# Picked columns of a graph network: who takes them out of PSUM, and how many there are

## The chip, the cores and the metric

The kernel runs on one core of a Trainium2 chip. The time is the device time of one execution in microseconds (us). Five engines work side by side, each through its own list of instructions in order: TensorE (PE) multiplies matrices into PSUM, VectorE (DVE) and ScalarE (ACT) work on PSUM and SBUF, GpSimd (POOL) issues here nothing but indirect DMAs, and SyncE (SP) issues the plain DMAs. They wait for each other by semaphores.

## The reference

Four graph networks run one after the other over one graph with 12,500 nodes and 412,500 edges, and after each comes a residual sum and a layer norm:

```
x = LN(x + L0(x))   # sum of x[src] * edge_weight * weight over the edges of each dst
x = LN(x + L1(x))   # twice: message = (MLP(edge_attr) as a 16x16 matrix) @ h[src], mean over dst, GRU cell
x = LN(x + L2(x))   # two attention layers (3 heads, 1 head): softmax over the edges of each dst
x = LN(x + L3(x))   # two relational layers, 8 edge types, mean per type
```

The edges are sorted by dst. Every layer therefore needs the rows of a node table at the edges' sources (`table[src]`), multiplies them by something of the edge, and sums them over runs of equal dst.

## The kernel before

The edges lie as 128 partitions x 3,224 columns. They are passed over seven times (`k` = 0 to 6: L0; L1 twice; L2 twice; L3 twice), each time in 62 chunks (`c`) of `TC` = 52 columns. In each pass the rows of the node table at the sources of a chunk come into `gb` in two ways:

- Most columns, `TC - OFF[k]` of them, are **gathered**: POOL issues one indirect DMA a column (`gathers`, L532), which fetches one table row for each partition.
- The last `OFF[k]` columns are **picked**. The node table lies packed in SBUF: a 32-bit word of a node's value and a word of extra bits, as bf16 halves (`pack`). For one column PE multiplies a one-hot matrix (which of 128 node groups the source lies in) with the packed table, 7 matmuls for each part of the table, into a buffer of PSUM (`pick_words`, L768). The result holds the words of 14 neighbouring nodes. DVE multiplies it by a mask that is 1 at the node wanted (`keep_words`, L1160 for tables in two parts and L1164 for one) and writes bf16 halves to `xT48` / `xT16` / `xT32`; a sum over the 14 finishes the pair of columns (`place_words` L1170, `node_words` L1194), and `decode` restores the values. The masks are made once a chunk (`word_masks`, L1144).

Columns are picked in pairs `n` of two columns `u`. In pass 0 the one-hot matrices are computed, 4 of 7 groups by DVE (`code`, L1131) and 3 by ACT (`code_far`, L639 and L642), and most are stored in DRAM (`oh_d`); passes 1 to 6 load them from there, one DMA of 448 KB a pair (`load_onehots`, L375). `KEPT` is how many pairs of a chunk are stored.

DVE then does the sums of the chunk, one scan for each value (`sums`, L1284), and between the scans it does the picks of the *next* chunk. How many picks stand before which scan is set by shares: `until(c, f)` is the number of pick steps that are due when the fraction `f` of chunk `c` is done. PE's loop in the message network (`message_net`) and SP's loads use the same shares. PE fills up to three buffers of PSUM ahead (two halves of one buffer in passes 1 and 2) and waits on `d_keep`, which DVE raises with each column kept. POOL waits on `d_gbfree` for a free half of `gb`, and every fifth gather on `d_keep`, so that it is never more than about two columns ahead of DVE's share of the chunk (`LEAD` = 2).

In the typed passes 5 and 6 each pair goes on: DVE writes its node rows (`d_row`), PE transposes them (`turn_pair`, L808 and L809), ACT copies them out (`row_copy`, L657), PE multiplies by the matrices of the eight types (`typed_product`, L799), and in pass 5 ACT copies the result (`typed_out`, L664). In passes 3 and 4 ACT has one exponential a chunk (`exp_edges`, L650); in passes 1 and 2 it makes the hidden units of the edge network (`hidden_units`, L627). In pass 0 POOL also issues 4 x 49 look-ups of another search (`find`, L519).

## Time and profile before

| | |
|---|---|
| median of the timed runs | 22,273.71 us (22,271.88 to 22,275.55, three runs) |
| span of the profiled execution | 30,666.4 us |
| PE busy | 19,689.1 us (64%), 89,726 matmuls |
| DVE busy | 18,344.5 us (60%) |
| ACT busy | 2,899.0 us (9%) |
| POOL busy | 16,237.0 us (53%) |

The profiled execution is the only one whose instructions are known; the result lists no time for it beside its span. It is 8,393 us longer than the median of the runs that were timed without a profile. Durations of single instructions and their order are read from it; how much each engine idles in it is not the same as in a timed run. In the rows, a name like `xT<-psB,sub` says what an instruction writes and reads, "idle before" is the time that the engine stood still in front of it, and what follows the arrow is what ended that.

### The profile page before, as it was taken

Reading aid. Unit: us, or ns where it says so; the run is one execution under the profiler, and the core shown is the slowest. Engines: PE = TensorE matmul, PEld = TensorE weight load, DVE = VectorE, ACT = ScalarE, POOL = GpSimd, SP = SyncE. Lnnn points to the kernel's source line nnn. Section 1 sums busy time; section 2 is a strip of 40 time slices with the busy share of each in tenths; the row PEclk is TensorE's granted clock in tenths of the full one; section 3 lists DMA queues with packets and bytes.
Section 4 is the critical chain, followed back from the end, with each engine's and each line's share of the span. In section 5 each row is a group of like instructions: output and inputs, shape, how many; then the busy total and the mean of one; then the engine's idle time right before and its main releaser. Section 6 shows DMA issues by size and latency. Waiting matters only on the chain.

```text
span 30666.4 us, 276253 instructions
## 1 busy us (share of the span) xinstructions
PE 19689.1 (64%) x89726; PEld 9475.3 (31%) x89726; DVE 18344.5 (60%) x38447; ACT 2899.0 (9%) x6609; POOL 16237.0 (53%) x16846
## 2 busy tenths in 40 slices
PE   4466657767567776455555477777566665777775
PEld 1122223333223333233333233333333333333332
DVE  6566657777567777456666465555455554555554
ACT  3344400000000000100000000000000000000000
POOL 5555555555455555445555555555355554454555
PEclk8788878888778888677777688888688886888887
DMA  3333322222122222133333122222233332222221
GB/s 122 83 103 104 101 52 66 68 66 66 45 62 68 66 68 67 32 85 88 85 86 91 45 77 76 76 76 76 62 93 93 93 91 66 55 55 55 56 56 44
DMA packets 1271680, 2237.21 MB, mean 73 GB/s; under 512 B 386665, under 2 KB 737274, under 8 KB 1261818
## 3 DMA queue, kind: packets, MB, share of 16 engines
q1 hardware_dynamic: 729380, 2025.85, 19.9%
q0 software_dynamic: 538944, 192.26, 6.7%
q8 instruction: 744, 12.19, 0.2%
q14 instruction: 670, 5.49, 0.1%
q10 hardware_dynamic: 1942, 1.43, 0.0%
HBM read 1597.46 MB, written 620.66 MB: 72 GB/s over the span
## 4 chain that ended last, share of the span: by engine, by line
DVE 36%; another core or an unknown queue 27%; PE 22%; DVEq 7%; issue 7%; POOL 1%; DMA 0%; ACT 0%; ACTq 0%; SPq 0%; POOLq 0%
PE psB L768 17%; DVE Sb L1284 6%; DVE xT L1164 5%; DVE prod L1325 5%; DVE xT L1160 4%; DVE sub L1170 4%; DVEq L1169 3%; PE psB L839 2%; DVE prod L1328 1%; DVEq L1193 1%; DVE arena L1131 1%; DVEq L1324 1%; PE psB L905 1%; PE psA L799 1%
## 5 line engine op out<-in xcount | busy, mean ns | idle before, releaser
L768 PE MATMUL psB<-xp,arena 128*128 128x476 bf16 x26040 | 6949.8, 421 | 3618.6 <-DVE xT L1164 2521.8
L768 PEld LDWEIGHTS psB<-xp,arena 128*128 128x128 bf16 x26040 | 2630.0, 108 | 7599.1 <-issue 5550.5
L768 PE MATMUL psB<-ext,arena 128*128 128x308 bf16 (+1 forms) x17388 | 3670.7, 366 | 1826.4 <-issue 1114.7
L1160 DVE TENSOR_TENSOR xT<-psB,XT 128x616 bf16<-128x616 f32 (+1 forms) x1860 | 1803.2, 977 | 3128.9 <-remote 2508.0
L532 POOL DMA_INDIRECT gb<-tab3b,typi x2356 | 2269.1, 963 | 2348.7 <-DVE xT L1160 1489.5
L532 POOL DMA_INDIRECT gb<-tab1b,srci x2356 | 2293.3, 973 | 1929.0 <-issue 645.4
L532 POOL DMA_INDIRECT gb<-tab1a,srci x2356 | 2297.1, 975 | 1905.3 <-issue 651.3
L532 POOL DMA_INDIRECT gb<-tab2a,srci x2232 | 2111.8, 946 | 2047.6 <-DVE xT L1160 1350.0
L532 POOL DMA_INDIRECT gb<-tab2b,srci x2356 | 2229.3, 946 | 1789.9 <-DVE xT L1160 1043.6
L1164 DVE TENSOR_TENSOR xT<-psB,sub 128x476 bf16<-128x476 f32 x2976 | 1920.1, 646 | 2039.8 <-remote 1670.1
L532 POOL DMA_INDIRECT gb<-tab3a,typi x2108 | 2093.8, 993 | 1897.2 <-DVE xT L1164 1015.9
L768 PEld LDWEIGHTS psB<-ext,arena 128*128 128x128 bf16 x17388 | 1791.3, 105 | 3674.4 <-issue 2432.4
L1325 DVE TENSOR_TENSOR prod<-psB,gb 128x1024 f32<-128x1024 f32 x1612 | 1974.6, 1225 | 1512.9 <-remote 1245.8
L839 PE MATMUL psB<-w2as,hid 64*128 64x256 f32 x12896 | 2119.9, 451 | 1132.1 <-DVE prod L1325 603.1
L532 POOL DMA_INDIRECT gb<-in_x,srci x1984 | 1891.0, 953 | 1655.5 <-DVE xT L1164 1011.3
L768 PE MATMUL psB<-ext,hid 128*128 128x308 bf16 (+1 forms) x8652 | 1842.0, 365 | 959.4 <-issue 575.5
L768 PE MATMUL psB<-arena,ext 128*128 128x476 bf16 x8120 | 1887.5, 389 | 798.5 <-DVE xT L1160 681.4
L1170 DVE TENSOR_REDUCE sub<-xT 128x34 f32<-128x476 f32 (+2 forms) x2418 | 1882.3, 778 | 227.0 <-issue 8.4
L839 PEld LDWEIGHTS psB<-w2as,hid 64*128 64x128 f32 x12896 | 1325.2, 214 | 2131.6 <-issue 1539.8
L1328 DVE TENSOR_REDUCE prod<-prod 128x64 f32<-128x1024 f32 x1488 | 1798.9, 1209 | 0.0
L1284 DVE TENSOR_TENSOR_SCAN Sb<-psA,Sb,prod 128x52 f32<-128x52 f32 x6588 | 1675.0, 313 | 17.2 <-issue 0.4
L1164 DVE TENSOR_TENSOR xT<-psB,arena 128x476 bf16<-128x476 f32 x1116 | 678.1, 642 | 1371.6 <-remote 1128.7
(337 smaller groups left out, 19385.5 us busy)
## 6 DMA issues: line engine op xcount, KB each, us to landing
arena<-oh_d SPq DMA_DIRECT2D x1861, 448.0 KB
hid<-oh_d SPq DMA_DIRECT2D x639, 448.0 KB
oh_d<-arena SPq DMA_DIRECT2D x558, 448.0 KB
ext<-oh_d SPq DMA_DIRECT2D x290, 448.0 KB
S2a<-Sb SPq DMA_DIRECT2D x62, 1404.0 KB
S2b<-Sb SPq DMA_DIRECT2D x62, 884.0 KB
ext<-in_attrT SPq DMA_DIRECT2D x404, 128.0 KB
S3a<-Sb SPq DMA_DIRECT2D x62, 832.0 KB
```

The costliest lines, as they stand in the source:

```text
L532: pool.indirect_dma_start(gb[:, o:o + width], None, table, at(idx[:, t:t + 1])).then_inc(l_gat[k][c % 2], 16)
L768: m = pe.matmul(psB[b][:, o:o + W], pk.onehot(n)[:, g, u * P:(u + 1) * P], pk.part(g, q).bitcast(BF16), start=g == 0, stop=g == NB - 1)
L799: t = pe.matmul(outs[u], pk.xT[0:K, o + u * P:o + (u + 1) * P], pk.mats, start=True, stop=True)
L839: m = pe.matmul(psB[g % 2][:, to:to + 256], hid[64 * u:64 * u + 64, o:o + P], w2as[64 * u:64 * u + 64, 256 * u:256 * u + 256], start=True, ...
L905: m = pe.matmul(psB[made % 3][:, to:to + width], xT[0:K + ones, o + i * P:o + (i + 1) * P], W, start=True, stop=True)
L1160: v.tensor_tensor(to.rearrange("p (b f x) -> p b f x", b=2, x=2 * JB), psB[b][:, :].rearrange("p (b w) -> p b w", b=2)[:, :, 0:W].rearrang ...
L1164: v.tensor_tensor(v3(to, 2 * JB), v3(psB[b][:, u * 512:u * 512 + W], 2 * JB), spots, ALU.mult).then_inc(d_keep, 1)
L1169: v.drain()
L1170: v.tensor_reduce(found(pk)[:, 2 * i * U:2 * (i + 1) * U], v3(words_of(pk.k, n)[:, 0:2 * U * JB], JB), AX.X, ALU.add)
L1284: m = v.tensor_tensor_scan(now[:, :, q], decay(q), data(q), old[:, TC - 1, q:q + 1] if c else 0.0, ALU.mult, ALU.add)
L1325: m = v.tensor_tensor(pr[i % 2], psB[g % 2][:, :].rearrange("p (t o i) -> p t o i", t=4, o=16), bc(gv[:, 4 * i:4 * i + 4, :], 2, 16), ALU. ...
L1328: v.tensor_reduce(msg[:, 4 * i - 4:4 * i, :], pr[(i - 1) % 2], AX.X, ALU.add)
```

## The change

1. `OFF` goes from (20, 14, 14, 16, 14, 18, 14) to (20, 16, 16, 20, 14, 20, 14): in passes 1, 2, 3 and 5 more columns of a chunk are picked and fewer gathered. `KEPT` goes with it from 9 to 10, and `oh_d` becomes two DRAM tensors, for even and odd chunks.
2. ACT copies each picked column from PSUM to SBUF as bf16 (`lift_words`), in all passes. PE now waits on ACT's semaphore `a_lift` for a free buffer. ACT waits for the pick (`t_pick`) and, at a pair's first column, until DVE has summed the pair before the last (`d_place`).
3. DVE masks both columns of a pair in one operation in SBUF, in place (`keep_pair`), and raises `d_keep` by 2. The masks become bf16.

```
-OFF = (20, 14, 14, 16, 14, 18, 14)
+OFF = (20, 16, 16, 20, 14, 20, 14)
...
+            def lift_words(pk, done, to):
+                W, two = 2 * JB * pk.units, len(pk.groups) == 2
+                size = W * len(pk.groups)
+                for s in range(done, min(to, 2 * pk.last)):
+                    n, u = divmod(s, 2)
+                    b = pk.slots[s % len(pk.slots)]
+                    word = words_of(pk.k, n).bitcast(BF16)[:, u * size:(u + 1) * size]
+                    if u == 0 and n >= 2:
+                        a.wait_ge(d_place, pk.place0 + n - 1)
+                    a.wait_ge(t_pick, pk.call0 + s + 1)
+                    if two:
+                        a.activation(word.rearrange("p (b w) -> p b w", b=2), psB[b][:, :].rearrange("p (b w) -> p b w", b=2)[:, :, 0:W],
+                                     ACT.Copy).then_inc(a_lift, 1)
+                    else:
+                        a.activation(word, psB[b][:, u * 512:u * 512 + W], ACT.Copy).then_inc(a_lift, 1)
+                return max(done, to)
...
                 for c in range(NCH):
+                    done = lift_words(pk, done, pk.until(c, 0.45) - 2)
                     a.wait_ge(d_zz, NCH * (k - 3) + c + 1)
                     a.activation(psA[1][:, 0:2 * TC * H], da, ACT.Exp).then_inc(a_exp, 1)
...
                 if s >= free:
-                    pe.wait_ge(d_keep, pk.call0 + s - free + 1)
+                    pe.wait_ge(a_lift, pk.lift0 + s - free + 1)
                 pick_words(pk, n, u).then_inc(t_pick, 1)
...
-                return v3(tile[:, o:o + pk.off * 2 * JB], 2 * JB)
+                return v3(tile[:, o:o + pk.off * JB].bitcast(BF16), 2 * JB)
...
-            def keep_words(pk, n, u):
...
-                v.wait_ge(t_pick, pk.call0 + 2 * n + u + 1)
...
-                    v.tensor_tensor(v3(to, 2 * JB), v3(psB[b][:, u * 512:u * 512 + W], 2 * JB), spots, ALU.mult).then_inc(d_keep, 1)
+            def keep_pair(pk, n):
+                U, i = pk.units * len(pk.groups), n % pk.pairs
+                word = words_of(pk.k, n).bitcast(BF16)[:, 0:4 * U * JB].rearrange("p (u f x) -> p u f x", u=2, x=2 * JB)
+                v.wait_ge(a_lift, pk.lift0 + 2 * n + 2)
+                if i == 0:
+                    v.drain()
+                v.tensor_tensor(word, word, bc(spot_masks(pk)[:, 2 * i:2 * i + 2, :], 2, U), ALU.mult).then_inc(d_keep, 2)
...
-                v.tensor_reduce(found(pk)[:, 2 * i * U:2 * (i + 1) * U], v3(words_of(pk.k, n)[:, 0:2 * U * JB], JB), AX.X, ALU.add)
+                v.tensor_reduce(found(pk)[:, 2 * i * U:2 * (i + 1) * U], v3(words_of(pk.k, n)[:, 0:2 * U * JB], JB), AX.X, ALU.add).then_inc(d_place, 1)
```

The calls of `lift_words` stand in ACT's loops where the picks are due: in pass 0 a pair is copied after the codes of the next one, in passes 1 and 2 the hidden units and the copies follow PE's order, in passes 3 and 4 the copies run up to two columns short of the share at which the exponential stands, and in passes 5 and 6 they come ahead of the row copies.

DVE's list in pass 1, where the picks of the next chunk stand between the products of this one (1024 elements a product; `xT` holds the picked words, `sub` the masks). Before:

```order
L1325 TENSOR_TENSOR prod<-psB,gb 128x1024 [waits t_weight]
L1328 TENSOR_REDUCE prod<-prod 128x64
L1164 TENSOR_TENSOR xT<-psB,sub 128x476 [waits t_pick]
L1170 TENSOR_REDUCE sub<-xT 128x34
L1325 TENSOR_TENSOR prod<-psB,gb 128x1024 [waits t_weight]
L1328 TENSOR_REDUCE prod<-prod 128x64
L1164 TENSOR_TENSOR xT<-psB,sub 128x476 [waits t_pick]
```

And after:

```order
L1361 TENSOR_TENSOR prod<-psB,gb 128x1024 [waits t_weight]
L1364 TENSOR_REDUCE prod<-prod 128x64
L1202 TENSOR_TENSOR xT<-xT,sub 128x952 [waits a_lift]
L1208 TENSOR_REDUCE sub<-xT 128x34
L1361 TENSOR_TENSOR prod<-psB,gb 128x1024 [waits t_weight]
L1364 TENSOR_REDUCE prod<-prod 128x64
L1361 TENSOR_TENSOR prod<-psB,gb 128x1024 [waits t_weight]
```

Each product had an operation on one column behind it; now every second one has an operation on two columns, which waits for ACT and not for PE.

ACT's list in pass 0, where it computes three groups of the one-hot matrices of a pair (squares to `hid`, then the codes to `arena`). Before:

```order
L639 ACTIVATE hid<-arena,cst 128x256 [waits l_kept0,t_pick,l_key0]
L639 ACTIVATE hid<-arena,cst 128x256 x2
L642 ACTIVATE arena<-hid,cst 128x256 x3
L639 ACTIVATE hid<-arena,cst 128x256 [waits l_kept1,t_pick,l_key1]
L639 ACTIVATE hid<-arena,cst 128x256 x2
L642 ACTIVATE arena<-hid,cst 128x256 x3
```

And after:

```order
L681 ACTIVATE hid<-arena,cst 128x256 [waits l_kept0,t_pick,l_key0]
L681 ACTIVATE hid<-arena,cst 128x256 x2
L684 ACTIVATE arena<-hid,cst 128x256 x3
L647 ACTIVATE xT<-psB 128x476 [waits t_pick,d_place]
L647 ACTIVATE xT<-psB 128x476 [waits t_pick]
L681 ACTIVATE hid<-arena,cst 128x256 [waits l_kept1,t_pick,l_key1]
L681 ACTIVATE hid<-arena,cst 128x256 x2
L684 ACTIVATE arena<-hid,cst 128x256 x3
```

Between the codes of two pairs stand now two copies, which wait for PE's picks of the pair before and for DVE's sums of the pair before the last.

## Rows read from the trace of the kernel before

**Rows 1.** The page, part 1: busy us, share of the span, instructions.
```profile
PE 19689.1 (64%) x89726; PEld 9475.3 (31%) x89726; DVE 18344.5 (60%) x38447; ACT 2899.0 (9%) x6609; POOL 16237.0 (53%) x16846
```
**Rows 2.** The gathers, a row for each pass: ns min/median/max, first and last start.
```profile
L532 POOL DMA_INDIRECT gb<-tab1a,srci x2356: 942/947/2581, 3991.3 to 8141.0; - x197
L532 POOL DMA_INDIRECT gb<-tab1b,srci x2356: 942/947/2594, 8429.5 to 12540.9; - x197
L532 POOL DMA_INDIRECT gb<-tab2b,srci x2356: 941/947/1216, 17537.9 to 21555.9; - x197
L532 POOL DMA_INDIRECT gb<-tab3b,typi x2356: 942/947/1762, 25996.7 to 30472.9; - x197
L532 POOL DMA_INDIRECT gb<-tab2a,srci x2232: 942/947/1341, 12991.7 to 17149.9; - x186
L532 POOL DMA_INDIRECT gb<-tab3a,typi x2108: 941/947/2562, 21948.1 to 25705.9; - x192
L532 POOL DMA_INDIRECT gb<-in_x,srci x1984: 942/947/2638, 32.6 to 3792.3; - x199
```
**Rows 3.** Timeline of POOL, pass 0: start, us, what; three equal rows left out.
```profile
2004.59 0.95 POOL L532 DMA_INDIRECT gb<-in_x,srci  x1 [0.30 <-issue]
...
2009.60 0.95 POOL L532 DMA_INDIRECT gb<-in_x,srci  x1 [0.31 <-issue]
```
**Rows 4.** Stretches of passes 1, 3, 5, 6: length; PE, PEld, DVE, ACT, POOL busy; clock.
```profile
3990.00:8180.00 4190.00, 2891.01 (x13330) 1319.70 (x13330) 2985.80 (x4075) 276.09 (x403) 2297.13 (x2356) 0.82 0.25 65
...
12991.00:17200.00 4209.00, 2431.72 (x13894) 1442.54 (x13894) 2564.58 (x7029) 27.52 (x66) 2116.92 (x2238) 0.78 0.31 86
...
21948.00:25760.00 3812.00, 2420.23 (x11242) 1320.25 (x11242) 2196.11 (x6085) 330.43 (x1123) 2115.62 (x2131) 0.81 0.32 91
25996.00:30510.00 4514.00, 3190.28 (x14758) 1506.66 (x14758) 2339.37 (x4281) 162.00 (x434) 2274.87 (x2362) 0.83 0.21 55
```
**Rows 5.** The same view, two short stretches of pass 1.
```profile
5000.00:5010.00 10.00, 9.63 (x57) 4.55 (x53) 9.67 (x11) 0.00 (x0) 7.13 (x8) 1.00 0.26 67
5010.00:5018.00 8.00, 3.15 (x15) 1.89 (x15) 2.60 (x3) 0.69 (x1) 4.73 (x5) 0.80 0.06 6
```
**Rows 6.** Groups of DVE by line and shape: passes 0, 1, 3, 3, 6.
```profile
L1131 DVE TENSOR_SCALAR arena<-arena,cst 128x256 bf16<-128x256 f16 x2480 | 542.6, 297 | 1.0 <-DMA arena<-key_d 1.0
...
L1164 DVE TENSOR_TENSOR xT<-psB,sub 128x476 bf16<-128x476 f32 x868 | 559.4, 645 | 364.5 <-remote 312.8 <-issue 24.4 <-PE psB L768 22.4
...
L1160 DVE TENSOR_TENSOR xT<-psB,XT 128x616 bf16<-128x616 f32 x992 | 771.4, 787 | 1525.0 <-remote 1233.4 <-PE psB L768 215.8 <-issue 71.2
...
L1144 DVE TENSOR_TENSOR XT<-hlk,cst 128x448 f32<-128x448 bf16 x62 | 38.8, 626 | 25.3 <-DMA x<-xn2a,pcoi 20.8
...
L1160 DVE TENSOR_TENSOR xT<-psB,ext 128x952 bf16<-128x952 f32 x868 | 953.9, 1141 | 54.6 <-remote 39.3 <-PE psB L768 10.8
```
**Rows 7.** Timelines of DVE and of POOL in pass 1, the same moment.
```profile
5031.26 3.37 DVE L1284 TENSOR_TENSOR_SCAN Sb<-same,Sb,prod 128x52 f32<-128x52 f32 x15
...
5033.16 2.28 POOL L532 DMA_INDIRECT gb<-tab1a,srci  x1 [0.30 <-issue]
```
**Rows 8.** Groups of ACT by line and shape: passes 0, 5, 5.
```profile
L639 ACT ACTIVATE hid<-arena,cst 128x256 bf16<-128x256 f16 x1860 | 808.2, 497 | 1996.0 <-issue 1426.8 <-remote 200.5 <-PE psB L768 191.4
...
L657 ACT ACTIVATE xT<-psA 128x256 f32<-128x256 f32 x558 | 213.6, 383 | 471.4 <-remote 288.9 <-PE psA L809 129.7 <-issue 49.9
...
L664 ACT ACTIVATE gb<-psA 128x64 f32<-128x64 f32 x558 | 125.1, 224 | 2977.3 <-remote 1748.3 <-PE psA L799 1096.3 <-issue 132.7
```
**Rows 9.** Timeline of PE in passes 3 and 5, picks only and the turn's wait.
```profile
14031.08 3.85 PE L768 MATMUL psB<-ext,hid 128*128 128x308 bf16 x28
...
24095.51 2.98 PE L768 MATMUL psB<-xp,arena 128*128 128x476 bf16 x14
...
24099.33 0.33 PE L808 MATMUL psA<-cst,arena 128*128 128x128 f32 x1 [0.48 <-DVE arena L1258]
...
24099.61 2.98 PE L768 MATMUL psB<-xp,hid 128*128 128x476 bf16 x14
```

More of the change, by code:

```diff
@@ L254, in gnn_program @@
             sem(f"d_{n}") for n in ("first", "zero", "key16", "find", "count", "cum", "ends"))
-        d_code, d_keep, d_row, d_typed, d_gbfree, d_sum, d_product, d_xe, d_zz = (
-            sem(f"d_{n}") for n in ("code", "keep", "row", "typed", "gbfree", "sum", "product", "xe", "zz"))
+        d_code, d_keep, d_place, d_row, d_typed, d_gbfree, d_sum, d_product, d_xe, d_zz = (
+            sem(f"d_{n}") for n in ("code", "keep", "place", "row", "typed", "gbfree", "sum", "product", "xe", "zz"))
         d_fix, d_fixexp, d_fixrow, d_input, d_evac, d_mid, d_act, d_block, d_stage, d_nodes = (
@@ L620, in exp_fix, with hidden_units, hidden @@
                 return exps + 1
-            def hidden_units(rep):
-                for h in range(NH):
+            def lift_words(pk, done, to):
[14 more added lines that the diff above has]
+                return max(done, to)
+            def hidden_units(rep, pk):
+                def hidden(h):
                     a.wait_ge(t_hidden, NQ * rep + h // 2 + 1)
@@ L627, in hidden_units @@
                     a.activation(hid[:, (h % 2) * 512:(h % 2 + 1) * 512], psA[h % 2][:, :], ACT.Relu, bias=b1s[:, 0:1]).then_inc(a_hid, 1)
+                hidden(0)
+                hidden(1)
+                done = lift_words(pk, 0, pk.until(-1, 1))
+                for c in range(NCH):
+                    for i in range(TC // 4):
+                        g = c * (TC // 4) + i + 1
+                        if g % 2 == 0 and g // 2 + 1 < NH:
+                            hidden(g // 2 + 1)
+                        done = lift_words(pk, done, pk.until(c, 0.9 * i * 4 / TC))
+                    done = lift_words(pk, done, pk.until(c, 1))
             def code_far(pk):
                 one = cst[:, C8 + 1:C8 + 2]
-                for n in range(pk.last):
+                for n in range(pk.last + 1):
+                    if n == pk.last:
+                        lift_words(pk, 2 * n - 2, 2 * n)
+                        break
                     far = [hid[:, (n % 2) * 512 + i * P:(n % 2) * 512 + (i + 1) * P].bitcast(BF16) for i in range(FAR)]
@@ L643, in code_far @@
                     m.then_inc(a_code, 1)
+                    if n:
+                        lift_words(pk, 2 * n - 2, 2 * n)
             def exp_edges(k):
```

61 lines of the change are left out of this document (29 added, 32 removed).

## The prediction, made before the changed kernel ran

> **What bounds the kernel now.** I read the totals of the page first, then the gathers pass by pass, then the stretches of each pass, then single rows in time order.
>
> The profiled execution spans 30,666.4 us and the median of the timed runs is 22,273.7 us: the profiled one is 8,393 us longer, so its idle time can't be taken at face value. [Rows 2] say where the span goes: from the first to the last gather of the seven passes it is 3,759.7 + 4,149.7 + 4,111.4 + 4,158.2 + 4,018.0 + 3,757.8 + 4,476.2 = 28,431.0 us, and 2,235.4 us lie outside these stretches. [Rows 3] show what POOL needs when nothing holds it: four gathers further is 5.01 us later, so 1.2525 us a gather (0.95 busy and 0.30 between). There are 15,748 gathers in the seven passes (the counts of [rows 2]) and, in pass 0, 196 look-ups of `find` on the same queue: 15,944 x 1.2525 = 19,970 us. With the 2,235.4 us outside, 22,205 us. That is 69 us under the median. So in the runs that are timed POOL issues gathers nearly without a break, and what is longer in the profiled execution is something else.
>
> [Rows 5] show what. In a full stretch PE and DVE are both busy for over 9.6 of 10 us at clock 1.00. In the next 8 us PE is busy for 3.15, and DVE, ACT and then POOL wait for it. Such holes come back in every chunk; PE waits there for nothing the trace names. With POOL alone accounting for 22,205 of 22,274 us, the timed runs have no room for them. I therefore take durations from the profile and no idle time. [Rows 1] agree in kind: POOL is busy for 53% of a span that is a third too long.
>
> Next to POOL stands DVE. A chunk is 52 edge columns, 62 chunks a pass. POOL needs (52 - OFF) x 1.2525 us for one: 40.1, 47.6, 47.6, 45.1, 47.6, 42.6, 47.6 us. DVE is busy in pass 1 for 2985.8 / 62 = 48.2 us a chunk, in pass 3 for 41.4, in pass 5 for 35.4 [rows 4]. In passes 1 and 2 the two are level: 0.6 us x 124 chunks = 74 us, which is about the 69 us that were over.
>
> **The change part by part.** *Fewer gathers.* OFF rises by 2 in passes 1, 2 and 5 and by 4 in pass 3: 10 gathers less a chunk, 620 in all, 620 x 1.2525 = 777 us of POOL. POOL per chunk is then 40.1, 45.1, 45.1, 40.1, 47.6, 40.1, 47.6. All of it counts as long as no other engine needs more than that: 22,274 - 777 = 21,497 us if nothing else comes late.
>
> *DVE: two reads of PSUM become one pass over SBUF.* The old operation takes 0.645 us for 476 elements, 0.787 for 616 and 1.141 for 952 [rows 6], that is 1.042 ns an element and 0.149 us fixed. The new one handles both columns, 952 elements in passes 1, 2, 5 and 0, 1,232 in pass 3, all of 16 bits and in SBUF. No row shows a 16-bit operation with two tensors in SBUF. Upper bound: the old rate, 1.14 and 1.43 us. The other side: the 16-bit comparison of L1131 takes 0.297 us for 256 elements [rows 6], so 0.58 ns an element, which gives 0.70 and 0.86 us. I take the lower one, since L1131 is the only row whose operands are of this kind. The Trainium skill (VectorE: DVE Perf Modes, The perf-mode tier table) says that a tensor_tensor does two elements a cycle when all is 16-bit in SBUF, and one with any operand in PSUM; by it the new operation would take 0.65 us, some 0.4 us less a chunk than I sum with. No row here shows it.
>
> Sums of DVE a chunk: pass 1 and 2, 48.2 - 14 x 0.645 + 8 x 0.70 + 0.65 for one more reduction = 45.4 (upper bound 49.0). Pass 3, 41.4 - 16 x 0.787 + 10 x 0.86 + 2 x 0.80 = 39.0 (44.7). Pass 5, 35.4 - 18 x 0.645 + 10 x 0.70 + 1.6 for one more pair's reduction and small operations = 32.4 (36.8). In passes 0, 4 and 6 DVE gets shorter and nothing else moves, since POOL sets their length.
>
> *ACT: the copies.* 256 elements take 0.383 us and 64 take 0.224 [rows 8]: 0.83 ns an element, so 0.57 us for 476 and 0.68 for 616. The tightest place is pass 0, where ACT also codes: 2 x 1.30 for six operations (L639's busy time over 620 pairs, 808.2 / 620 = 1.30 for three; the three of L642 have the same size) + 2 x 0.57 = 3.74 us a pair, 37.4 a chunk of 10 pairs, against 40.1 of POOL. Queued behind a copy that waits for its pick are the next pair's codes; PE needs 14 x 0.213 = 2.98 us for a pair [rows 9], so the pick is over before ACT has done the 3.2 us of work that stand between. Its cover is 2.7 us a chunk; it costs nothing as long as the semaphores between take under 0.27 us a pair.
>
> *PE: more columns.* Pass 3 goes from 224 to 280 matmuls a chunk; 28 take 3.85 us [rows 9], so 30.8 us becomes 38.5 against 40.1. Pass 1: 215 matmuls a chunk [rows 4] at 9.63 / 57 us [rows 5] are 36.3, with 14 more of 0.21 39.3 against 45.1. Pass 5: a pair takes 4.10 us [rows 9], from the start at 24095.51 to that at 24099.61, 0.48 of which PE waits for DVE. The DVE's share of a pair falls by 2 x 0.645 - 0.70 = 0.59 us, so I take 3.6 us and 36 a chunk; with the wait as now it would be 41.0 against 40.1.
>
> *Waits added.* PE now waits for ACT where it waited for DVE, and DVE works on a pair after a 0.57 us copy. Behind DVE's wait stand the scans of the chunk, behind those `d_gbfree` and POOL. ACT may be two pairs ahead of DVE, so this latency is hidden except in pass 5, where it is in the comparison above. POOL's own wait on `d_keep` now steps by two columns: one column later at odd counts, about 2 us, against a lag of two columns that is allowed.
>
> *Sum.* 22,274 - 777 = 21,497. In the four passes whose OFF rises another engine now stands within 1.6 us of POOL: DVE 45.4 beside 45.1 twice, PE 38.5 and DVE 39.0 beside 40.1, PE 36 to 41 beside 40.1. What such a tie costs is what it cost before: 69 us over 124 chunks, 0.56 us each. 4 x 62 x 0.56 = 139 us. Forecast 21,636, rounded 21,640 us.
>
> **The rivals.**
> *B, nothing ties:* 21,497 us. For it: the sums of DVE and PE are at or under POOL everywhere but by 0.3 us. Against: passes 1 and 2 paid for less.
> *C, the new operation runs at one element a cycle:* DVE 49.0 a chunk in passes 1 and 2 against 48.2 before, +100 us; pass 3 44.7 against 45.1, -25; pass 5 still POOL's, -155. 22,194 us. For it: the masks are repeated along one dimension, and no row shows the fast rate.
> *D, the other side, the new operation holds POOL up:* it reads two tensors in SBUF where the old one read one. [Rows 7]: while fifteen scans with two and three SBUF operands run without a break for 3.37 us, a gather takes 2.28 us and not 0.95. The Trainium skill (SBUF — State Buffer, Who interferes with whom) has the rule: such an instruction shares a read port with GpSimd's reads, and the second one waits to the end of the first. If each of the 3,720 new operations held POOL for its whole length, some 0.65 to 1.2 us, POOL would grow by 2,900 us: 24,400 us. It decides from (777 - 139) / 3,720 = 0.17 us each. Against: the masks' own operation L1144 reads two tensors in SBUF for 0.63 us once a chunk [rows 6], and the gathers of pass 3 have a median of 947 ns and none over 1,341, where the pass with the bursts has one of 2,581 [rows 2]; a single operation as short as this seems to fit between two reads.
> *E, PE at the recorded clock:* at the 0.78 to 0.82 of [rows 4] a matmul of pass 3 costs 2431.7 / 13,894 = 0.175 us, 280 of them 49.0 a chunk, +242 us on 45.1; pass 1 (2891.0 / 13,330 = 0.217 us each, 229 of them) 49.7 on 47.6, twice +130; 22,776 us. Against: [rows 5] show clock 1.00 where PE is busy and less only in and behind holes, and at that pace pass 6 would need 3190 / 62 = 51.5 us already now, which the median has no room for.
>
> **How the numbers follow.** Forecast 0.62 (21,500 to 21,800), B 0.18, C 0.08, D 0.07, E 0.05. The time is the forecast's, 21,640 us. The range reaches down past B by the 0.2% that a measurement of this kernel can't tell from no change, and up to ties of 1.8 us a chunk in place of 0.56 (248 x 1.8 = 450 over B), which takes in a pass 0 that ACT's copies stretch by 2 us a chunk (124 us): 21,450 to 21,950, which leaves out C, D and E, 0.20. Faster: forecast, B and two thirds of C, 0.85. Within 0.2%: 0.04, from C and E. Slower: D and the rest, 0.11.
>
> **What would show it.** In the profile after: gathers at 1.25 us where nothing holds them, 32 a chunk in passes 3 and 5 and 36 in 1 and 2. The pair operation at 0.65 to 0.70 us for 952 elements; at 1.14 it is C. Gathers over 2 us in passes 3 and 4, or a median that leaves 0.947, would be D. ACT copies of 0.57 us. DVE busy under 2,830 us in pass 1. The profiled span itself may grow, since PE has 6,076 pick matmuls more (98 a chunk) to pass through its holes; that would not make the forecast wrong. Wrong is it if the median is over 21,950 or the pair operation is not the shorter one.

## The result, and the profile after

The changed kernel takes 22,350.6 us (median of 4 runs, 22,341.5 to 22,389.8) where the kernel before takes 22,274.6 (4 runs, 22,271.9 to 22,284.3): a ratio of 1.0039, 95% interval 1.0027 to 1.0051. It is slower by 76 us. The forecast was 21,640 us, 634 less than before, and the range ended at 21,950. Rival D is the side it came out on; it had 0.07.

One fact is needed to read the numbers. The runs fell on chips of two kinds. On one kind (four of the six chips of the experiments) the kernel before takes 22,225 to 22,284 us at a granted clock of 0.90, and a profiled execution takes as long as a timed one. On the other (two) it takes 30,466 to 30,704 us in every run, profiled or not, at a granted clock of 0.80, and PE issues its matmuls with the holes of [rows 5]. Why they differ, and whether it belongs to the chip or to its state in those hours, no run shows: no chip was seen in both ways. The profile of before that the forecast rests on (30,666 us, clock 0.80) is like those of the second kind; the times and the profile of after are of the first. A profile of before from the first kind (run i1_before below, span 22,236.0 us) is the one that after is set against here. Each ratio compares runs on one chip; profiles are also compared across chips of one kind, where the same kernel differs by some 60 us (after: 22,340 to 22,398).

The page of after, span and part 1 (busy us, share, instructions), and the chain that ended last:

```profile
span 22340.0 us, 302277 instructions
## 1 busy us (share of the span) xinstructions
PE 18361.3 (82%) x96174; PEld 9645.2 (43%) x96174; DVE 16441.4 (74%) x35905; ACT 7721.6 (35%) x14173; POOL 16555.9 (74%) x16226
...
POOL 41%; DVE 16%; PE 16%; issue 14%; DVEq 6%; DMA 5%; ACT 2%; ACTq 0%; SPq 0%; POOLq 0%
```

The same lines of before, on this kind of chip:

```profile
span 22236.0 us, 276253 instructions
## 1 busy us (share of the span) xinstructions
PE 17574.0 (79%) x89726; PEld 9002.1 (40%) x89726; DVE 18287.6 (82%) x38447; ACT 2915.9 (13%) x6609; POOL 16235.0 (73%) x16846
...
POOL 29%; DVE 26%; PE 23%; issue 12%; DVEq 7%; DMA 3%; ACT 0%; ACTq 0%; POOLq 0%; SPq 0%
```

DVE lost 1,846 us of work and POOL has 620 gathers less, yet POOL is busy 321 us longer and its share of the chain goes from 29% to 41%. So a gather has become longer. The gathers of after (ns min/median/max, first and last start), the rows that answer to [rows 2]:

```profile
L543 POOL DMA_INDIRECT gb<-tab2b,srci x2356: 941/947/1977, 12651.6 to 15893.7; - x197
L543 POOL DMA_INDIRECT gb<-tab3b,typi x2356: 940/947/1914, 19023.4 to 22163.2; - x197
L543 POOL DMA_INDIRECT gb<-tab1a,srci x2232: 941/947/3534, 3100.4 to 6078.5; - x186
L543 POOL DMA_INDIRECT gb<-tab1b,srci x2232: 941/947/3532, 6271.5 to 9257.9; - x186
L543 POOL DMA_INDIRECT gb<-in_x,srci x1984: 939/947/2637, 32.8 to 2941.2; - x199
L543 POOL DMA_INDIRECT gb<-tab2a,srci x1984: 939/947/1572, 9584.9 to 12354.9; - x199
L543 POOL DMA_INDIRECT gb<-tab3a,typi x1984: 941/947/2659, 16193.6 to 18852.1; - x199
```

and those of before on this kind of chip:

```profile
L532 POOL DMA_INDIRECT gb<-tab1a,srci x2356: 938/944/2526, 3021.2 to 6177.9; - x197
L532 POOL DMA_INDIRECT gb<-tab1b,srci x2356: 938/944/2524, 6373.4 to 9524.2; - x197
L532 POOL DMA_INDIRECT gb<-tab2b,srci x2356: 940/944/1189, 12950.7 to 15898.8; - x197
L532 POOL DMA_INDIRECT gb<-tab3b,typi x2356: 938/944/1798, 19089.4 to 22059.2; - x197
L532 POOL DMA_INDIRECT gb<-tab2a,srci x2232: 940/944/1397, 9854.4 to 12653.7; - x186
L532 POOL DMA_INDIRECT gb<-tab3a,typi x2108: 940/944/2654, 16199.8 to 18917.9; - x192
L532 POOL DMA_INDIRECT gb<-in_x,srci x1984: 938/944/2642, 32.9 to 2862.7; - x199
```

The median moved by 3 ns; what grew is a tail, which the median hides. Pass 4 (tab2b) is where to look: its counts of picked columns and of gathers are the same, and from first to last gather it went from 2,948.1 to 3,242.1 us. Summed over every gather (what each takes over 947 ns; called lengthening below) it is 8 us there before and 297 after; in all seven passes 312 and 1,185.

Stretch from first to last gather in us, and lengthening behind the slash:

| pass | before (i1) | after | difference | forecast |
|---|---|---|---|---|
| 0 in_x | 2,829.7 / 36 | 2,908.4 / 77 | +79 | 0 |
| 1 tab1a | 3,156.7 / 76 | 2,978.1 / 155 | -179 | -120 |
| 2 tab1b | 3,150.8 / 67 | 2,986.4 / 163 | -164 | -120 |
| 3 tab2a | 2,799.3 / 10 | 2,770.0 / 120 | -29 | -276 |
| 4 tab2b | 2,948.1 / 8 | 3,242.1 / 297 | +294 | 0 |
| 5 tab3a | 2,718.1 / 86 | 2,658.5 / 178 | -60 | -120 |
| 6 tab3b | 2,969.8 / 29 | 3,139.8 / 194 | +170 | 0 |
| outside | 1,663.5 | 1,656.6 | -7 | 0 |

(forecast: gathers saved x 1.2525 us, less 35 us for the tie of a pass.) The differences make +104 us, the spans 22,340.0 - 22,236.0 (the medians on one chip differ by 76). The passes with 620 gathers less give back 432 us; the three in which no gather was saved lose 543.

What lengthens a gather is seen in pass 4. Timeline of DVE in after (start, us, what, idle time before it):

```profile
14024.52 0.22 DVE L1424 TENSOR_TENSOR psA<-psA,same 128x52 f32<-128x52 f32 x1 [0.47 <-ACT psA L696]
...
14024.76 1.88 DVE L1427 TENSOR_TENSOR prod<-gb,psA 128x1664 f32<-128x1664 f32 x1
14027.35 1.21 DVE L1202 TENSOR_TENSOR xT<-xT,XT 128x2016 bf16<-128x2016 bf16 x1 [0.29 <-ACT xT L644]
14028.65 1.20 DVE L1208 TENSOR_REDUCE sub<-xT 128x72 f32<-128x1008 f32 x1
14033.30 1.21 DVE L1202 TENSOR_TENSOR xT<-xT,XT 128x2016 bf16<-128x2016 bf16 x1 [1.04 <-ACT xT L644]
14034.60 1.20 DVE L1208 TENSOR_REDUCE sub<-xT 128x72 f32<-128x1008 f32 x1
```

and of POOL in the same moment:

```profile
14025.13 0.95 POOL L543 DMA_INDIRECT gb<-tab2b,srci  x1 [0.30 <-issue]
14026.38 0.94 POOL L543 DMA_INDIRECT gb<-tab2b,srci  x1 [0.30 <-issue]
14027.63 1.75 POOL L543 DMA_INDIRECT gb<-tab2b,srci  x1 [0.30 <-issue]
14029.68 0.95 POOL L543 DMA_INDIRECT gb<-tab2b,srci  x1 [0.30 <-issue]
14030.93 0.94 POOL L543 DMA_INDIRECT gb<-tab2b,srci  x1 [0.30 <-issue]
14032.18 0.95 POOL L543 DMA_INDIRECT gb<-tab2b,srci  x1 [0.31 <-issue]
14033.43 1.89 POOL L543 DMA_INDIRECT gb<-tab2b,srci  x1 [0.30 <-issue]
```

The pair operation (L1202, `xT<-xT,XT`, two tensors in SBUF) runs from 14033.30 to 14034.51. The gather that starts at 14033.43, in it, takes 1.89 us; so does the one at 14027.63, with 1.75. The gather at 14025.13 starts in an operation of 1.88 us that has one operand in PSUM, and takes 0.95. Taken over the pass: in 412 of the 434 pair operations a gather starts, on average 850 ns before their end, and is 706 ns longer than 947. In pass 6 it is 427 of 434, 537 ns before the end, 419 ns longer. A held gather is longer by what is left of the operation, less about 0.13 us. A gather that is already running when the operation starts is 1 ns longer (174 cases in pass 4), or not at all (376 in pass 6). In before, the masks out of PSUM of the same two passes meet 1,566 starts of gathers (795 + 771), and those gathers take 944 ns, as the median does.

The pair operation isn't the only one that holds. Put down to the operation in which the gather starts, 744 of the 1,185 us fall on it: 37, 27, 29, 111, 291, 71 and 179 us in passes 0 to 6. In passes 1 and 2 most falls on the scans (`Sb<-same,Sb,prod`, which run without a break), 120 and 127 us, where before had 74 and 65. In pass 4, POOL and its issue times are 99% of the chain, so each held us there is a us of time: 289 more of lengthening, 294 of time.

The groups of after that the forecast had put a price on (ns min/median/max; L1202 by the tiles of passes 0 to 2, 3 and 4, and 6; pass 5 has 620 more; L647 a copy of 476 elements):

```profile
L1202 DVE TENSOR_TENSOR xT<-xT,sub x1612: 617/653/730, 131.5 to 9263.4; 128x952 bf16<-128x952 bf16 x180
L1202 DVE TENSOR_TENSOR xT<-xT,XT x1054: 729/800/1280, 9595.4 to 15875.0; 128x1232 bf16<-128x1232 bf16 x104, 128x2016 bf16<-128x2016 bf16 x72
L1202 DVE TENSOR_TENSOR xT<-xT,ext x434: 1137/1141/1165, 19034.3 to 22144.7; 128x1904 bf16<-128x1904 bf16 x145
L647 ACT ACTIVATE xT<-psB x4464: 540/567/570, 128.4 to 18843.0; 128x476 bf16<-128x476 f32 x195
```

### The profile page after: what moved, and what is told of

It reads as the page before. It is cut to its first block, busy times and chain, and to the rows that moved or that the text cites. A ratio compares the mean times of both kernels' runs of the same rounds, so it can differ in the third digit from the quotient of the medians.

```text
span 22340.0 us, 302277 instructions
## 1 busy us (share of the span) xinstructions
PE 18361.3 (82%) x96174; PEld 9645.2 (43%) x96174; DVE 16441.4 (74%) x35905; ACT 7721.6 (35%) x14173; POOL 16555.9 (74%) x16226
## 4 chain that ended last, share of the span: by engine, by line
POOL 41%; DVE 16%; PE 16%; issue 14%; DVEq 6%; DMA 5%; ACT 2%; ACTq 0%; SPq 0%; POOLq 0%
POOL gb L543 38%; PE psB L817 8%; PE psB L888 5%; DVE prod L1361 4%; DVE Sb L1320 3%; DVEq L1207 3%; DVE xT L1202 2%; POOL ext L558 2%; DVE sub L1208 2%; PE psB L954 1%; DVEq L1360 1%; DMA gb<-tab2a,srci 1%; DMA gb<-tab3a,typi 1%; PE psA L876 1%; POOL ext L530 1%
## 5 line engine op out<-in xcount | busy, mean ns | idle before, releaser
L817 PE MATMUL psB<-xp,arena 128*128 128x476 bf16 x28364 | 6435.0, 378 | 980.4 <-DVE arena L1180 971.2
L644 ACT ACTIVATE xT<-psB 128x616 bf16<-128x616 f32 (+2 forms) x2976 | 2548.3, 861 | 6260.9 <-PE psB L817 4588.2
L647 ACT ACTIVATE xT<-psB 128x476 bf16<-128x476 f32 x4464 | 2456.9, 562 | 5902.8 <-PE psB L817 5436.7
L817 PE MATMUL psB<-ext,arena 128*128 128x308 bf16 (+1 forms) x19712 | 3495.3, 339 | 603.9 <-DMA arena<-oh_d 597.4
L543 POOL DMA_INDIRECT gb<-tab2b,srci x2356 | 2525.1, 1072 | 718.3 <-issue 718.0
L543 POOL DMA_INDIRECT gb<-tab3b,typi x2356 | 2422.8, 1028 | 744.6 <-issue 717.7
L817 PEld LDWEIGHTS psB<-ext,arena 128*128 128x128 bf16 x19712 | 1967.6, 100 | 2083.0 <-DMA arena<-oh_d 639.2
L543 POOL DMA_INDIRECT gb<-tab2a,srci x1984 | 1997.1, 1007 | 774.3 <-issue 584.2
L888 PE MATMUL psB<-w2as,hid 64*128 64x256 f32 x12896 | 1953.7, 424 | 673.6 <-DVE prod L1361 671.0
L1208 DVE TENSOR_REDUCE sub<-xT 128x34 f32<-128x476 f32 (+2 forms) x2666 | 2061.3, 773 | 247.2 <-issue 5.3
L1202 DVE TENSOR_TENSOR xT<-xT,sub 128x952 bf16<-128x952 bf16 x1612 | 1047.8, 650 | 593.7 <-ACT xT L647 576.7
```

The lines of the kernel that those rows point to most:

```text
L543: pool.indirect_dma_start(gb[:, o:o + width], None, table, at(idx[:, t:t + 1])).then_inc(l_gat[k][c % 2], 16)
L644: a.activation(word.rearrange("p (b w) -> p b w", b=2), psB[b][:, :].rearrange("p (b w) -> p b w", b=2)[:, :, 0:W], ACT.Copy).then_inc(a_l ...
L647: a.activation(word, psB[b][:, u * 512:u * 512 + W], ACT.Copy).then_inc(a_lift, 1)
L817: m = pe.matmul(psB[b][:, o:o + W], pk.onehot(n)[:, g, u * P:(u + 1) * P], pk.part(g, q).bitcast(BF16), start=g == 0, stop=g == NB - 1)
L888: m = pe.matmul(psB[g % 2][:, to:to + 256], hid[64 * u:64 * u + 64, o:o + P], w2as[64 * u:64 * u + 64, 256 * u:256 * u + 256], start=True, ...
L1202: v.tensor_tensor(word, word, bc(spot_masks(pk)[:, 2 * i:2 * i + 2, :], 2, U), ALU.mult).then_inc(d_keep, 2)
```

## The experiments

Lengthening is as above. Some expectations have counts wrong: there are 3,720 pair operations in all (g1_one_input and j2_split name the 1,612 of passes 0 to 2), 55 a chunk with the old counts (e2_old_off has 53), no gather is saved in pass 6 (h2_off_only), and the old counts are those given here (i2_old_off names others). "New counts" are 16, 16, 20, 20 picked columns over tab1a, tab1b, tab2a, tab3a; "old counts" 14, 14, 16, 18.

**1. Chips of the slower kind (before 30,589 and 30,611 us).** Four kernels on one chip, then the same four on another: before again; the pair operation with one input; the copies at the old counts; the new counts without copies.

```
- v.tensor_tensor(word, word, bc(spot_masks(pk)..., 2, U), ALU.mult).then_inc(d_keep, 2)
+ v.tensor_reduce(into, v3(words_of(pk.k, n)[:, 0:2*U*JB], JB), AX.X, ALU.add).then_inc(d_keep, 2)   # one_input
- OFF = (20, 16, 16, 20, 14, 20, 14)
+ OFF = (20, 14, 14, 16, 14, 18, 14)                                                                # old_off
+ LIFT = ()    # off_only: in no pass a ScalarE copy; VectorE masks out of PSUM as before
```

> The changed kernel with the masking of a pair replaced by a sum over the same words, which reads one tensor in SBUF and not two and lasts as long (0.65 us for 952 halves, 0.8 for 1,232, 1.2 for 2,016); the masking is left out. Waits, copies, picks and gathers stay. Theory lock (the pair operation reads two tensors in SBUF and holds POOL's gathers): gathers over their 0.947 us fall from 1,185 us in sum to some 300, as before, and the time falls by 800 to 900 us to about 21,500. Rival traffic (310 more loads of 448 KB slow the gathers) and rival chain (the detour over ScalarE paces the passes): the time stays at 22,350 and the gathers stay long.

> The changed kernel with OFF as before (20, 14, 14, 16, 14, 18, 14): copies by ScalarE and pair masking, without the 620 gathers less. Theory lock: 53 pair operations a chunk still hold POOL, the floor is 777 us higher, and only the ties of passes 1 to 3 with DVE and PE go: 22,800 to 22,950 us, gathers long by about 1,050 us in sum. Rival chain or traffic: it is the added columns that cost, so at most 22,275 us.

> OFF as changed, the picked columns masked out of PSUM by DVE as before (no copies by ScalarE; masks in bf16). Theory lock: gathers stay near 0.95 us (under 300 us too long in sum), and DVE ends the passes 1 to 3: two more columns of 0.645 and a reduction of 0.65 are +1.9 us a chunk in passes 1 and 2, in pass 3 +4.7 on 41.4, pass 5 gains 1.6: 22,300 to 22,500 us. Rival traffic: gathers as long as in the changed kernel, 1,185 us in sum.

| | ratio, first chip | second chip | lengthening |
|---|---|---|---|
| one input | 0.9813 (0.9777 to 0.9849) | 0.9818 (0.9771 to 0.9865) | 376, 356 |
| copies, old counts | 0.9650 (0.9605 to 0.9696) | 0.9614 (0.9546 to 0.9681) | 793, 812 |
| new counts only | 0.9668 (0.9632 to 0.9704) | 0.9666 (0.9615 to 0.9718) | 291, 293 |
| before again | 30,704 us | 30,571 us | 310, 298 |

Before again was to show whether the holes of PE belong to one execution, and was expected near 22,275 us. They don't: it took 30,704. The three forecasts were made for chips of the other kind, and none of their times came. The lengthening goes with the two-input operation here too, but the time doesn't go with the lengthening. Each change alone makes the kernel 3.3 to 3.9% faster where PE has the holes, and slower where it hasn't (below). The changed kernel itself was not run on such a chip. These eight runs settle nothing about the time of the result; each kernel was run again on the other kind.

**2. The changed kernel on another chip of the faster kind.**

> The changed kernel itself, beside the kernel before on the same chip. The first comparison (22,351 against 22,275 us) and the last four runs (before at 30,589 us without a profile) show that one program has two paces by chip, and that the holes of PE in the first profile were real for its chip. If before takes 30,600 us here, the chip is of the slow kind: by the sums of the other four kernels there (masking left out -1.9%, old OFF -3.5%, OFF alone -3.3%) the changed kernel then takes 28,800 to 30,000 us, so it is faster where PE has holes and slower where it has none. If before takes 22,275 us, this repeats 22,351 us.

22,382.3 us against 22,232.3, ratio 1.0067 (1.0044 to 1.0089), lengthening 1,222. It was run once more beside experiment 7 (k2_changed): 22,369.9 against 22,249.7, 1.0053 (1.0036 to 1.0069), lengthening 1,212. The result stands.

**3. One input in place of two.** The edit of experiment 1, on the faster kind.

> The changed kernel with its 1,612 masking operations on VectorE reading one tensor of SBUF (the pair) instead of two (pair and mask): same place, same count, about the same 0.65 us each (1.2 us for the 434 of pass 4); the masking itself is left out. Theory (a VectorE operation with two inputs in SBUF holds POOL's gather that meets it): the gathers' lengthening over 947 ns falls from 1,185 us to about 300 us, and on a chip where the kernel before takes about 22,270 us the time falls by 700 to 850 us, to 21,500 to 21,650 us. Rival 1 (the gathers' lengthening lies beside other waits, the chain of ScalarE, VectorE and PE sets the end): lengthening falls, time stays at 22,300 to 22,380 us. Rival 2 (the hold has nothing to do with the second input): lengthening stays near 1,185 us and the time at 22,350 us.

21,652.9 us against 22,232.8, ratio 0.9742 (0.9726 to 0.9758), lengthening 396: the Theory, 3 us over its range and 96 over its lengthening, and both rivals are out. What is summed lasts as long (0.649, 0.776 and 1.198 us in passes 0, 3 and 4). In pass 4 a gather starts in 416 of these operations, with 558 ns of them left, and takes 944 ns. The gathers of passes 4 and 6:

```profile
L543 POOL DMA_INDIRECT gb<-tab2b,srci x2356: 940/944/1274, 12519.0 to 15466.6; - x197
L543 POOL DMA_INDIRECT gb<-tab3b,typi x2356: 940/944/1793, 18512.2 to 21475.6; - x197
```

Pass 4 is back at 2,947.6 us, pass 6 at 2,963.4. By passes 0 to 6 the stretches are shorter than in after by 2, 16, 7, 108, 294, 85 and 176 us, 688 in all, and 688 is what the spans differ by (22,340.0 - 21,652.4). So the second input costs the changed kernel 0.69 ms, and without it the kernel is 2.6% faster than before. The sum also writes less than the mask does (34 elements for a pair of 952), but that isn't the cause: the masks of before out of PSUM write as much as the pair operation, and gathers that start in them take 944 ns. The 84 us of lengthening over before lie in passes 1 and 2 (79 us), where gathers start in the scans. That the time comes so near to the forecast (21,640) is in part luck. It is 580 us under before on its chip, where 634 were forecast; passes 1 and 2 win 366 us instead of 240, and passes 0 and 3 together 61 instead of 276.

**4. Each half alone, and the halves where they pay.** h1_mix has the new counts, and the copies and the pair operation in passes 1, 2 and 3 only; in the others PE waits for `d_keep` as before.

```
+ LIFT = (1, 2, 3)
  def lift_words(pk, done, to):
+     if pk.k not in LIFT: return max(done, to)
  def keep_pair(pk, n):
+     if pk.k not in LIFT: ...  # keep_words of before, out of PSUM
```

> The changed kernel with the ScalarE copies and the masking of pairs in SBUF in passes 1, 2 and 3 only, where a masking operation is 0.65 to 0.8 us long; in passes 0, 4, 5 and 6 VectorE masks out of PSUM as in the kernel before, at the new counts of picked columns. Theory (hold of a gather by a VectorE operation with two inputs in SBUF, dearer the longer it is): the lengthening of the gathers in passes 0, 4, 5 and 6 falls from 77 + 297 + 178 + 194 us to 15 to 100 us each, some 500 us in all, and the time on a chip where the kernel before takes 22,232 us is 21,750 to 21,900 us, against 22,380 for the changed kernel. Rival 1 (the ScalarE copy chain, not the hold, is the price, and passes 1 to 3 carry it): 22,200 to 22,400 us. Rival 2 (masking out of PSUM in passes 5 and 6 makes VectorE the bound there, as in the kernel before): 22,000 to 22,200 us.

> The new counts of picked columns (16 over tab1a and tab1b, 20 over tab2a and tab3a) with the kernel before's masking out of PSUM by VectorE everywhere, no ScalarE copy. Theory (POOL's gathers at 1.25 us each set the time; fewer gathers in passes 1, 2, 5 and 6, more masking on VectorE): the lengthening of the gathers stays near 290 us, 21,900 to 22,250 us where the kernel before takes 22,232: what gathers it saves is taken back in part by VectorE becoming late in passes 1 and 2 (masks at 1,141 to 1,200 ns for 16 columns). Rival 1 (VectorE is the bound in passes 1 and 2, and the copies are needed): 22,300 us and more. Rival 2 (nothing is taken back): 21,600 us.

> The changed kernel's ScalarE copies and its masking of pairs in SBUF, with the kernel before's counts of picked columns (12 over tab1a and tab1b, 14 over tab2a and tab3a). Theory (hold of gathers): lengthening near 800 us as on the other kind of chip, against 300 of before; what the hold adds, 500 us, is paid by the stretches that are at POOL's floor (passes 0, 4, 5 and 6, some 450 us): 22,400 to 22,700 us where the kernel before takes 22,250. Rival 1 (the chain through VectorE's masks out of PSUM bounds passes 1 to 3 in the kernel before, and the copies free it by more than the hold costs): 21,900 to 22,200 us. Rival 2 (nothing changes, since what bounds is neither): 22,250.

| | ratio | us / before | passes 0 to 6, us | lengthening |
|---|---|---|---|---|
| new counts only | 1.0105 (1.0088 to 1.0121) | 22,487.4 / 22,251.4 | 2,863 3,254 3,246 2,949 2,953 2,581 2,973 | 308 |
| copies, old counts | 1.0251 (1.0234 to 1.0268) | 22,784.9 / 22,233.6 | 2,887 3,056 3,075 2,914 3,243 2,826 3,136 | 1,145 |
| mix | 0.9775 (0.9759 to 0.9791) | 21,742.1 / 22,251.4 | 2,868 2,981 2,989 2,734 2,953 2,579 2,972 | 604 |

Each half alone loses more than both together. With new counts only, passes 1, 2 and 3 get longer by 97, 95 and 150 us although they have fewer gathers: DVE masks 2 and 4 columns more a chunk, and DVE leads the chain with 37%. My Theory there (up to 22,250) was too low; Rival 1 holds. With copies only, passes 1 and 2 win 101 and 76 us, where DVE was busy in before for 2,937 of 3,157 and 2,935 of 3,151 us, and all others lose, with 40 to 294 us more of lengthening each; the Theory was right in kind and 85 us short of the size. The mix came 8 us under the range of its Theory, with 604 us of lengthening where some 500 were expected. It takes the copies where DVE sets the pace and leaves them out where POOL does. Its passes 4 to 6:

```profile
L544 POOL DMA_INDIRECT gb<-tab2b,srci x2356: 940/945/1299, 12579.1 to 15531.7; - x197
L544 POOL DMA_INDIRECT gb<-tab3b,typi x2356: 940/945/1792, 18583.6 to 21555.3; - x197
...
L544 POOL DMA_INDIRECT gb<-tab3a,typi x1984: 940/945/2583, 15831.6 to 18410.8; - x199
```

It beats both kernels: 2.25% less than before, 2.8% less than the changed one on the same kind of chip.

**5. The kernel before on the faster kind of chip.**

> The kernel before, once more, for its profile on a chip where it takes about 22,250 us. Theory: the gathers' lengthening over 947 ns is near 300 us as on the other chips, and the time above POOL's floor (15,944 gathers at 1.2525 us, 19,970 us, plus 650 us at the ends of passes and 1,000 us of other stretches) lies in passes in which POOL waits. From the page: the span about 22,240 us and the time outside the seven gather stretches 1,500 to 1,700 us, not the 2,235 us that the earlier profile had. Rival: outside the gathers it is 2,235 us here too, and the stretches are at the floor; then the forecast's floor was right and the changed kernel lost elsewhere.

22,237.3 us, span 22,236.0. Outside the gathers' stretches it spends 1,663.5 us, not 2,235. The floor of all gathers and look-ups (19,970 us) leaves 603 us in the stretches: 206 and 200 in passes 1 and 2 (76 and 67 of them held gathers), 99 in pass 0, 78 in pass 5 (86 held), 4, -3 and 19 in passes 3, 4 and 6. The Theory holds, and its rival is out.

**6. Twice the operation in pass 4; half its length everywhere.**

```
  def keep_pair(pk, n):   # j1_twice
+     if pk.k == 4:
+         v.tensor_tensor(word, word, bc(spot_masks(pk)..., 2, U), ALU.mult)
+         v.drain()
      v.tensor_tensor(word, word, ...)

- v.tensor_tensor(word, word, ...).then_inc(d_keep, 2)      # j2_split
+ for u in range(2):
+     v.tensor_tensor(word[:, u], word[:, u], bc(spot_masks(pk)[:, 2*i+u, :], 1, U), ALU.mult).then_inc(d_keep, 1)
```

> The changed kernel with the masking of a pair done twice in pass 4 (434 more operations of 1.2 us on VectorE, which changes nothing in the values); VectorE is busy 57% of pass 4, so 520 us more of work have room. Theory (each such operation holds one gather for 0.68 us): the lengthening of the gathers in pass 4 goes from 297 to 550 to 600 us, its stretch from 3,242 to 3,500 to 3,550 us, the time from about 22,370 to 22,620 to 22,680 us. Rival (the loss of pass 4 is not the hold, but a later word on VectorE's path): the time grows by 0 to 60 us, or by the whole 520 us if VectorE's work is on the path.

> The changed kernel with each masking of a pair as two operations, one per column, of half the size (3,224 operations of about 0.35 us, 0.4 in pass 3, and 0.6 in pass 4, in place of 1,612 of 0.65, 0.8 and 1.2 us). Theory (an operation of length L holds the gather that meets it by up to its length, so its mean price goes by the square of L over twice the cadence of 1.25 us): lengthening of the gathers from 1,185 us to 750 to 900 us, of which pass 4 from 297 to 150 to 190; the time falls by 200 to 350 us, to 22,020 to 22,170 us. Rival 1 (a price for each operation, whatever its length): lengthening near 2,000 us and the time 22,900 us or more. Rival 2 (a price for each element read): no change, 22,370 us.

Twice: 22,276.3 us against 22,243.8 (1.0014, 1.0004 to 1.0023). That is not 250 to 310 us more than the changed kernel but 94 less (k2_changed on the same chip); pass 4 takes 3,160.7 us with 218 of lengthening, against 3,242.1 and 297. The Theory's sentence "each such operation holds one gather for 0.68 us" is refuted, and so are both forms of the rival. POOL in the profile of j1_twice:

```profile
14025.22 1.69 POOL L543 DMA_INDIRECT gb<-tab2b,srci  x1 [0.30 <-issue]
14027.22 0.98 POOL L543 DMA_INDIRECT gb<-tab2b,srci  x1 [0.30 <-issue]
...
14030.99 0.94 POOL L543 DMA_INDIRECT gb<-tab2b,srci  x1 [0.30 <-issue]
14032.24 0.94 POOL L543 DMA_INDIRECT gb<-tab2b,srci  x1 [0.30 <-issue]
14033.49 0.95 POOL L543 DMA_INDIRECT gb<-tab2b,srci  x1 [0.30 <-issue]
```

and the pair operations beside them:

```profile
14024.90 1.20 DVE L1203 TENSOR_TENSOR xT<-xT,XT 128x2016 bf16<-128x2016 bf16 x1
14026.17 1.21 DVE L1205 TENSOR_TENSOR xT<-xT,XT 128x2016 bf16<-128x2016 bf16 x1
...
14031.04 1.20 DVE L1203 TENSOR_TENSOR xT<-xT,XT 128x2016 bf16<-128x2016 bf16 x1
14032.31 1.21 DVE L1205 TENSOR_TENSOR xT<-xT,XT 128x2016 bf16<-128x2016 bf16 x1
```

Only a gather that starts during an operation is held. The first operation of the upper pair holds the gather that starts at 14025.22 with 0.88 us of it left: 1.69 us, 0.74 more than 0.947. That gather then goes on beside the second, and the next starts at 14027.22, 0.16 us before the second one ends. In the lower pair the gathers start at 14030.99 and 14032.24, each 0.05 to 0.07 us ahead of an operation, and none is held. Over the pass, gathers start in all 434 second operations, but 137 ns before their end, and are lengthened by 25 ns. An operation costs what is left of it when a gather starts, and by the time of the second one POOL is at work on its gather. Gathers also start in fewer of the first ones than in after (371, with 670 ns left, against 412 and 850); why is not shown.

Split: 22,138.1 us against 22,243.8 (0.9958, 0.9941 to 0.9974), 232 us under the changed kernel on this chip. The lengthening is 915 us in all and 118 in pass 4, where it was 297: less than expected there (150 to 190), a little more in sum (750 to 900). Passes 4 and 6 take 3,060.5 and 3,053.1 us instead of 3,242.1 and 3,139.8. Passes 1 and 2 get 33 and 27 us longer, since two operations of 0.399 us are 0.15 us more of DVE than one of 0.65. A price for each operation, or for each element, is out.

The Theory of the square holds only in sum (the part of the pair operations went from 744 to 381 us). Passes 0, 4 and 6 fell (77 to 52, 297 to 118, 194 to 111), passes 3 and 5 didn't (120 to 129, 178 to 183). The two halves stand directly behind each other, and a held gather can last past the first: in pass 3, 210 of the 253 gathers that start in a first half and are held go on to the end of the second, and are 389 ns longer on average with 518 ns left of both; in pass 5 it is 93 of 153. In j1_twice, where a `drain` stands between the two, none of the 371 lasted past the first. So a run of two-input operations without a gap can hold like one long operation, as the scans of [rows 7] do.

**7. Two inputs, or the double rate of 16-bit operands?** Experiment 3 took both away.

```
+ wide = words_of(pk.k, n)[:, 0:2*U*JB].rearrange("p (u f x) -> p u f x", u=2, x=JB)
+ v.tensor_tensor(wide, wide, bc(spot_masks(pk)[...].bitcast(F32), 2, U), ALU.mult).then_inc(d_keep, 2)
```

> The changed kernel with each of its 3,720 masking operations done on 32-bit words: the same bytes of the pair and of the masks, both in SBUF, half as many elements at one a cycle, so about the same 0.65 us for a pair of 952; the product is of the words and not of the two columns packed in them, so what is masked is not right. Theory A (two inputs in SBUF hold the gather that starts during them): lengthening 1,100 to 1,250 us, time within 0.5% of the changed kernel, 22,250 to 22,450 us where the kernel before takes 22,240. Theory B (it is the double rate of 16-bit operands that holds): lengthening near 400 us and 21,600 to 21,700 us, as with one input.

22,367.4 us, and 22,369.9 for the changed kernel beside it; lengthening 1,212 both. The operation has the length it had, on half as many elements:

```profile
L1203 DVE TENSOR_TENSOR xT<-xT,sub x1612: 617/653/728, 131.9 to 9283.7; 128x476 f32<-128x476 f32 x180
```

Theory A holds, B is out. It decides whether both operands of a VectorE operation lie in SBUF, and not the width of the elements.

## Why the prediction was wrong

**The step that failed is the dismissal of D.** The prediction named the mechanism, gave 0.17 us an operation as the point from which it decides, and set it aside with "a single operation as short as this seems to fit between two reads". Three things were wrong around it.
- *The evidence was a maximum and a median.* The median can't move while under half of the gathers are hit. And the longest gather of pass 3, 1,341 ns, was the hold itself: in that profile a gather starts in only 1 of the 62 L1144 of pass 3, with 0.52 us left, and it is this one (first two rows). The same trace had the clear case: L1415, once a chunk in pass 5, reads two tensors in SBUF (last two rows); gathers start in 60 of them and are 1.46 us longer.

```profile
12992.89 0.63 DVE L1144 TENSOR_TENSOR XT<-hlk,cst 128x448 f32<-128x448 bf16 x1 [20.80 <-DMA x<-xn2a,pcoi]
12992.99 1.34 POOL L532 DMA_INDIRECT gb<-tab2a,srci  x1 [0.30 <-issue]
...
22174.31 1.89 DVE L1415 TENSOR_TENSOR prod<-gb,wE 128x1664 f32<-128x1664 f32 x1
22174.68 2.35 POOL L532 DMA_INDIRECT gb<-tab3a,typi  x1 [0.30 <-issue]
```

- *The price was bounded by "all or nothing".* 2,900 us supposed that every operation holds for its length. By the rule that the prediction quoted, held from the gather's start to the operation's end, an operation of length L that is met at random costs L x L / (2 x 1.2525) us: 0.17 for 0.65, 0.52 for 1.14, 0.57 for 1.2 us. 2,232 x 0.17 + 620 x 0.25 (0.79 us) + 434 x 0.57 + 434 x 0.52 = 1,007 us of lengthening, an estimate; with the measured 0.13 us less in each hold it is 724. Measured are 744 us in the pair operations, 0.20 us each, and 688 us of time, 0.185 each. That is over the prediction's own limit of 0.17 us each, 638 in all.
- *Passes without a change in counts were taken as free.* "In passes 0, 4 and 6 DVE gets shorter and nothing else moves": nothing was to be won there, since POOL sets their length, so any price on POOL is a loss in full. They lost 79, 294 and 170 us, of which the second input is 2, 294 and 176.

The sign that the prediction named for D was set wrong too. It wanted gathers over 2 us in passes 3 and 4, or a median that leaves 0.947 us. The longest are 1,572 and 1,977 ns and the median stayed, and yet it was D: 0.947 and what an operation of 1.2 us can add, 1.2 - 0.13, is hardly over 2 us.

**The floor was taken from an execution of the other kind.** The step "the 2,235.4 us outside, 22,205 us, 69 us under the median" adds a time of the slower kind of chip to a floor for the faster (there 1,663.5). The sum fitted by chance: it is 19,970 + 1,663.5 + 603. With it fell "the timed runs have no room for holes": that was true of those chips, but it isn't the profiling that causes them. This didn't decide. Passes 1 and 2 stood 206 and 200 us over POOL's floor, not 37 each, so their gain was larger than forecast (343 against 240 us).

**Pass 3 was mis-sized.** DVE's sum of 39.0 us a chunk and PE's 38.5 are what the profile of g1_one_input shows: 2,372.0 / 62 = 38.3 and 2,412.3 / 62 = 38.9. But the chunk takes 2,661.8 / 62 = 42.9 us, not 40.1 + 0.56. Of the 247 us that pass 3 fell short, 108 are held gathers (experiment 3); 139 are left. The prediction had put nothing down for the loads of the one-hot matrices, and there the profile points: in pass 3 of g1_one_input PE waits 274 us for them (354 in after), they are 8.9% of the chain that ended last in that pass, and in pass 3 of before and of h2_off_only PE waits 31 us for them, once, for the first load. No run tried them apart, so this cause is not shown.

**Right were** the pair operation (0.65 us, where 0.70 was summed with; the Trainium skill's rule in VectorE: DVE Perf Modes, The perf-mode tier table, gave an estimate of 0.65, and the trace agrees with 0.653), the copies (0.567 for 0.57 us), the fewer gathers at 1.2525 us, and DVE's work (2,783 us in pass 1, forecast under 2,830). DVE's work was only not what was short.

**Pass 0** is 79 us longer, and 76 with one input, so this is not the hold. ACT is busy for 2,157 of its 2,908 us. The prediction gave its cover as 2.7 us a chunk, and 1.3 us a chunk were lost. In that pass DVE waits 502 us for ACT's copies, where it waited 83 us for PE's picks before; whether this is the loss was not tried (without copies pass 0 took 2,830 to 2,868 us, so up to half of it may be scatter).

The Trainium skill (SBUF — State Buffer, Who interferes with whom) says that a Vector instruction with two SBUF inputs contends with a GpSimd instruction that reads SBUF, that the port pair they share is an exclusive lock, and that the order of issue decides which of them waits. The runs agree: the gather reads its indices in SBUF, and one that starts second is longer by what is left of the operation, less 0.13 us (experiments 3 and 7). The other order, a VectorE operation that waits for a gather, doesn't show: L1202 keeps to 617 to 730 ns for 952 elements. The same section notes as inferred that a `tensor_tensor` doesn't stall descriptor generation; here it stalls the gather as a whole, by 706 ns on average in pass 4.
